# All orders of steps laid out anew, fills over 32 rows, and the latest producer's wait named first, in a four-layer block on one core

## The chip, the cores and the metric

The kernel runs on 1 core of one Trainium2 chip. The metric is the device time of one execution in microseconds, the median of several runs. A core has a matrix engine (TensorE, PE in the profile), a vector engine (VectorE, DVE), a scalar engine (ScalarE, ACT), a general one (GpSimd, POOL), and SyncE (SP), which here only issues DMAs. Each works off its own list of instructions in order; semaphores tie the lists together.

## The reference, cut to what matters

The input x has the shape (16, 64, 64, 256): 16 images of 4096 tokens of 256 values. Four layers follow each other, each on a group norm of x and added to x:

```python
def layer0(x, emb):             # codebook of 1024 vectors
    dis = sum(x*x, -1) + sum(emb*emb, 0) - 2 * x @ emb
    return take(emb.T, argmin(dis, -1))
def layer1(x):                  # within each row of 64 tokens
    f, g, h = x @ Wf + bf, x @ Wg + bg, x @ Wh + bh        # 32, 32, 256 wide
    return einsum('bhij,bhjo->bhio', sigmoid(f @ g.T), h)
def layer2(x):                  # n = 4096 tokens of an image
    x0, x1, x2 = x @ w1, x @ w2, x @ w3
    sm = softmax(x0[:, :, None] * x1[:, None, :], axis=1)
    return sigmoid(einsum('bn,bnm->bm', x2, sm)) * x
def layer3(x):                  # linear attention, 4 heads of 32
    q, k, v = split(x @ w_qkv)
    q, k = softmax(q, over the 32) * 32**-0.5, softmax(k, over tokens)
    out = einsum('context(k, v), q') @ w_out + b_out
    return (out - mean) * rsqrt(var + 1e-3) * gamma + beta
for layer in (layer0, layer1, layer2, layer3):
    x = x + layer(group_norm(x, groups=32))
```

## The kernel before

An image stays in SBUF as XT, 256 channels (two chunks of 128) by 4096 tokens, in 8 groups of 512 tokens. Loads, transposes in and out, the layers' work and the additions are small steps, each a Python function that issues one to a dozen instructions on one engine, waits for what it needs and raises a semaphore when done. A step is called as `exp(old, 7, 1)`: the image, then which piece of it.

**Orders.** For every engine the kernel holds a list of step calls, written out by hand: a prologue for the first image, a loop, and an epilogue. The loop body runs 15 times, with three images in flight: new is turned in, scored (layer 0), put through layer 1 and projected for layer 2; old has its layer 2 (the fills and exps), its gate and the start of layer 3; last gets the end of layer 3 and is sent out. Nothing but these lists decides what stands behind what on an engine; only waits for semaphores tie the engines to each other.

**Stages of one pass through the loop on PE.** First the fill stage: fills, sums, the end of layer 3 of last (final_out, L1515), and turn_in of new (L1273). Then the scoring stage, with fills of old between the scores. Then the gate of old and layer 1 of new, then layer 3 of old with the projection of new.

**Layer 0.** The group norm's factors come from gn(0) (PE L1258 and L1261, DVE, POOL). ACT norms a group (L551) and rounds it to fp16 as n_hi (L567), POOL makes the remainder n_lo (L435). score on PE is, per tile of 128 tokens and half of the codebook, six matmuls by the helper split (L1239: hi hi, hi lo, lo hi for two chunks). best on DVE (L896) adds the bias and takes the maximum of a half, index (L902) finds its place, POOL gathers the code vector (L441), PE turns it (L1297), DVE adds it (L908).

**Layer 1.** Per group ACT norms (L551) and rounds (L578), POOL makes the remainder (L448), PE does l1_fg (L1316), l1_h (by L1239), l1_scores (L1340) and l1_out (L1350), ACT copies fg (L586) and does the sigmoid by tanh (L591, L595), DVE copies h and adds (L916, L923).

**Layer 2.** project writes the three projections of an image as rows; they are split into bfloat16 pieces, 12 rows per quad of partitions that lie 32 apart. The tensors of pieces hold 32 rows per quad: rows 12 to 31 are set to zero at the start (L463, L465) and nothing writes them afterwards. A pair fill(h, 0), fill(h, 1) computes x0 times x1 for one tile and four quads of 512 tokens: two matmuls each (L1407), on 12 rows, the first step on quads 0 and 1, the second on quads 2 and 3. exp on ACT (L618) takes each half from PSUM; sums on PE (L1416) multiplies the four quads' exps with a stationary of 4 columns and gathers into PSUM. A part of the tiles goes by bexp on ACT (L629) and bsum on DVE (L992) instead. The last step is the gate (DVE L999, ACT L639 to L645, PE L1425, L1434).

**Layer 3.** Norm and rounding (ACT L551, L662; POOL L458), l3_qv and l3_k on PE (L1239), exp on ACT, l3_q on DVE (L1030, L1032), the turns on PE (L1461, L1471), the context (L1483). At the end final_out on PE (L1515) turns a group back, DVE (L1088, L1101) and ACT (L695) do the layer norm, POOL the root (L495).

**Waits.** A step names its waits one after the other ahead of its instruction. In the built program the first that is named rides on the instruction itself, and every further one is an instruction of its own ahead of it. In the orders shown below the last name in the brackets is the one that rides.

## Time and profile before

| what | us |
|---|---|
| median of 3 runs | 5465.11 (5464.95 to 5479.77) |
| profiled execution, its own time | 5467.99 |
| its span | 5466.2 |
| PE busy | 5123.3 |
| DVE busy | 4387.4 |
| ACT busy | 4037.1 |
| POOL busy | 1964.2 |
| mean granted clock of PE | 0.963 |

The span is what the profile covers; the execution's own time is 1.8 us more, and 2.9 us more than the median. Busy time is the sum of what an engine's instructions took, without its waits, and matmuls' ends are modelled, so a busy PE may be waiting for its clock. The granted clock is a share of 2.4 GHz. Times in the rows below are from the start of the span. The fifteen passes of the loop repeat about every 331 us; most rows are from one of them, from 2103 to 2434 us. In the rows of stretches each engine has its busy time and, in brackets, its instructions; behind POOL stand the granted clock, the DMA share and GB/s.

### The profile page before, as it was taken

How to read it: one execution, taken by the hardware profiler on the slowest of the kernel's cores; microseconds unless marked ns; L12 is line 12 of the kernel's file. 1: busy time of each engine (PE TensorE's matmuls, PEld its weight loads, DVE VectorE, ACT ScalarE, POOL GpSimd, SP SyncE). 2: the span in 40 equal slices, each digit the busy share in tenths (PEclk: the TensorE clock that was granted, in tenths of full speed). 3: DMA queues.
4: the chain of work that ended last, by engine and by line, in shares of the span. 5: the costliest groups of instructions: out<-in, count | busy, mean ns of one | idle time of the engine just before them, and what ended most of it. 6: DMA issues, size and time to landing. Idle time of an engine off the chain costs nothing.

```text
span 5466.2 us, 109580 instructions
## 1 busy us (share of the span) xinstructions
PE 5123.3 (94%) x42984; PEld 2689.9 (49%) x42984; DVE 4387.4 (80%) x9218; ACT 4037.1 (74%) x6279; POOL 1964.2 (36%) x1594
## 2 busy tenths in 40 slices
PE   7799999999999999999999999999999999999986
PEld 3436445363543646445363553645446464453624
DVE  8478797887878888797887978778798887978836
ACT  1477878678786877868778786787868778786785
POOL 4225143342423425143351423424244351433403
PEclk9899999999999999999999999999999999999988
DMA  2010201102021020211102021020211102011000
GB/s 76 29 37 12 75 27 57 42 7 81 20 71 32 25 65 14 74 29 44 52 8 80 22 67 36 21 66 17 71 32 37 56 11 77 26 62 38 12 31 32
DMA packets 167966, 227.84 MB, mean 42 GB/s; under 512 B 13793, under 2 KB 146657, under 8 KB 167457
## 3 DMA queue, kind: packets, MB, share of 16 engines
q1 hardware_dynamic: 142880, 153.70, 8.5%
q0 software_dynamic: 24576, 67.14, 4.2%
q8 instruction: 345, 5.65, 0.4%
q14 instruction: 165, 1.34, 0.1%
HBM read 153.55 MB, written 67.24 MB: 40 GB/s over the span
## 4 chain that ended last, share of the span: by engine, by line
PE 72%; DVE 13%; ACT 9%; issue 4%; DMA 1%; POOL 1%; DVEq 0%; SPq 0%; ACTq 0%; POOLq 0%
PE PS L1239 36%; PE PS L1416 14%; PE PS L1407 5%; PE PS L1350 3%; PE PS L1515 2%; PE PS L1273 2%; ACT big L618 2%; DVE work L896 2%; PE PS L1297 2%; DVE stats L878 2%; ACT n_x L551 2%; PE PS L1316 1%; DVE idx L902 1%; PE PS L1365 1%; ACT soft L618 1%
## 5 line engine op out<-in xcount | busy, mean ns | idle before, releaser
L618 ACT ACTIVATE big<-PS 128x1024 f32<-128x1024 f32 x1216 | 1207.5, 1028 | 384.7 <-PE PS L1407 350.8
L441 POOL DMA_INDIRECT quant_H<-emb_t,idx x512 | 509.0, 994 | 906.2 <-DVE idx L902 879.7
L1239 PE MATMUL PS<-e_hi,n_hi 128*128 128x512 f16 x2048 | 780.4, 381 | 16.5 <-DVE m L896 9.0
L1239 PE MATMUL PS<-e_lo,n_hi 128*128 128x512 f16 x2048 | 777.2, 379 | 0.0
L1239 PE MATMUL PS<-e_hi,n_lo 128*128 128x512 f16 x2048 | 777.2, 379 | 0.0
L618 ACT ACTIVATE soft<-PS 128x1024 f32<-128x1024 f32 x576 | 577.3, 1030 | 257.8 <-PE PS L1407 255.8
L1416 PE MATMUL PS<-big,w 128*4 128x512 f32 x4864 | 680.3, 646 | 0.0
L878 DVE BATCH_NORM_STATS2 stats<-XT 128x6 f32<-128x512 f32 x1024 | 652.9, 683 | 11.0 <-POOL XT L454 1.0
L902 DVE FIND_INDEX8 idx<-m,work 128x8 uint32<-128x1024 f32 x512 | 624.2, 1219 | 0.0
L1407 PE MATMUL PS<-rhs,lhs 12*128 12x512 bf16 x3584 | 522.8, 403 | 71.5 <-ACT big L618 35.6
L495 POOL TENSOR_TENSOR rstd<-rstd,mhalf 128x4 f32<-128x4 f32 x128 | 131.9, 1030 | 1123.1 <-DVE rstd L1091 1123.1
L896 DVE CUSTOM_DVE_ANT_0 work<-PS,e_bias 128x512 f32<-128x512 f32 x512 | 350.6, 685 | 163.7 <-PE PS L1239 162.5
L1407 PEld LDWEIGHTS PS<-rhs,lhs 12*128 12x128 bf16 x3584 | 126.8, 91 | 677.9 <-ACT big L618 242.2
L551 ACT ACTIVATE n_x<-XT,gt,gs 128x512 f32<-128x512 f32 x512 | 393.6, 806 | 72.9 <-DVE gt L873 70.5
L896 DVE CUSTOM_DVE_ANT_0 work<-PS,e_bias,m 128x512 f32<-128x512 f32 x512 | 379.4, 741 | 32.0 <-PE PS L1239 26.7
L1239 PE MATMUL PS<-qv_hi,o_both 128*128 128x256 f16 x2048 | 357.9, 273 | 21.6 <-DVE soft L1032 21.6
L1239 PEld LDWEIGHTS PS<-e_hi,n_hi 128*128 128x128 f16 x2048 | 199.4, 97 | 351.1 <-DVE m L896 123.8
L435 POOL TENSOR_TENSOR n_lo<-n_x,n_hi 128x1024 f16<-128x1024 f32 x128 | 273.6, 2137 | 259.3 <-ACT n_hi L567 258.2
L992 DVE CUSTOM_DVE_ANT_0 o_x<-o_x,o_both 128x1024 f32<-128x1024 f32 x256 | 311.5, 1217 | 61.8 <-ACT o_x L629 61.8
L454 POOL TENSOR_TENSOR XT<-XT,big 128x1024 f32<-128x1024 f32 x128 | 303.5, 2379 | 151.8 <-DVE big L999 149.9
L629 ACT ACTIVATE o_x<-o_both,negm,s 128x1024 f32<-128x1024 f32 x256 | 317.7, 1241 | 38.7 <-DVE bnum L992 38.7
L448 POOL TENSOR_TENSOR n_lo<-n_x,n_hi 128x1024 f16<-128x1024 f32 x128 | 273.4, 2136 | 160.7 <-ACT n_hi L578 160.7
(214 smaller groups left out, 11030.5 us busy)
## 6 DMA issues: line engine op xcount, KB each, us to landing
xin<-x SPq DMA_DIRECT2D x128, 512.0 KB, 4.3
out<-yout SPq DMA_DIRECT2D x128, 512.0 KB, 3.0
o_both<-rows_d SPq DMA_DIRECT2D x32, 512.0 KB, 7.1
quant_H<-emb_t,idx POOLq DMA_INDIRECT x512, 2.8
XT<-emb SPq DMA_DIRECT2D x1, 1024.0 KB, 6.1
rows_d<-n_hi SPq DMA_DIRECT2D x32, 4.0 KB
XT<-wh SPq DMA_DIRECT2D x1, 256.0 KB, 5.5
XT<-wqv SPq DMA_DIRECT2D x1, 256.0 KB, 5.6
```

What stands on the lines that cost most here:

```text
L441: nc.gpsimd.indirect_dma_start(quant[:, g % 2, u, :], None, emb_t, bass.IndirectOffsetOnAxis(ap=idx[:, t % (2 * GT), 0:1], axis=0),).then_ ...
L454: nc.gpsimd.tensor_tensor(here, here, gated[:, g % 2, :, :], ALU.add).then_inc(g_added.sem, 1)
L551: return nc.scalar.activation(dst, XT[:, im % 2, k, g, :], copy, scale=gs[:, layer, k:k + 1], bias=gt[:, layer, k:k + 1])
L618: nc.scalar.activation(E[h % 3][:, z * 1024:(z + 1) * 1024], bank(2 * z, 2), ACT.Exp).then_inc(exped.sem, 1)
L629: nc.scalar.activation(EB, x0_row, ACT.Exp, scale=s3[:, 1, t:t + 1], bias=negm[:, t:t + 1], accum_out=bden[:, i:i + 1]).then_inc(b_exped.s ...
L878: last = v.bn_stats(stats[:, layer, k, g, :], XT[:, im % 2, k, g, :])
L896: v.tensor_tensor_reduce(biased[:, t % 2, part], bank(5 + half), e_bias[:, part], 1.0, m8[:, t % 2, 0:1] if half else -BIG, ALU.add, ALU.m ...
L902: v.max_index(idx[:, t % (2 * GT), :], m8[:, t % 2, :], biased[:, t % 2, :]).then_inc(l0_indexed.sem, 1)
L992: v.tensor_tensor_reduce(EB, EB, x2_row, 1.0, 0.0, ALU.mult, ALU.add, bnum[:, i:i + 1]).then_inc(b_summed.sem, 1)
L1239: ins = mm(dst, a, b, start=first and j == 0, stop=last and j == 2)
L1407: ins = mm(bank(r), lhs[rr, t * P:(t + 1) * P], rhs[rr, f * GW:(f + 1) * GW], start=True, stop=True)
L1416: ins = mm(PS[32 * q:32 * q + 4, 4, :], w2[:, t, f, :], E[h % 3][:, q * 512:(q + 1) * 512], start=h == 0, stop=h == HALVES - 1, skip_group ...
```

## The change

Three things are changed.

1. Every list of step calls of the five engines, in prologue, loop and epilogue, is written in another order. The sets of steps stay the same.
2. fill takes 32 rows of each quad instead of 12. The added rows are the zeros of the pieces, so the result is the same.
3. In some sixteen steps the waits are named in another order, so that the one for the producer expected last is first and rides on the instruction; score waits for l0_lo only at the first tile of a group, instead of at every tile, which takes 384 waits off PE.

The diff of the steps, cut: where a step is not shown in full, one or two waits changed places in the same way. Of the lists one line stands for all.

```diff
@@ SP, loop
-                exp(old, 0, 0); rows_back(old); final_out(last, 1); final_out(last, 3); turn_in(new, 1)
+                exp(old, 0, 0); rows_back(old); turn_in(new, 1); final_out(last, 1); turn_in(new, 3)
...
@@ ACT, l0_norm
-                    act.wait_ge(*l0_scored.room(im, 2 * (g * GT + GT) - 1, 4 * GT))
                     act.wait_ge(*l0_xn.after(im, g))
+                    act.wait_ge(*l0_scored.room(im, 2 * (g * GT + GT) - 1, 4 * GT))
@@ ACT, l1_norm
-                act.wait_ge(*l1_hed.room(im, 2 * g + 1, 4))
                 act.wait_ge(*l1_xn.after(im, g))
+                act.wait_ge(*l1_hed.room(im, 2 * g + 1, 4))
@@ ACT, l3_norm (l3_qved.room) and l3_qv (l3_ctxed.room): behind the other wait
...
@@ DVE, best
                 if half == 0:
+                    dve.wait_ge(*l0_scored.after(im, 2 * t))
                     dve.wait_ge(*l0_indexed.room(im, t, 2))
                 else:
                     dve.wait_ge(*l0_maxed.after(im, 2 * t))
-                dve.wait_ge(*l0_scored.after(im, 2 * t + half))
+                    dve.wait_ge(*l0_scored.after(im, 2 * t + 1))
@@ DVE, gating (g_normed), qsoft (l3_qturned.room), l3_q (l3_qsoft.room), final_sq (f_sq)
...
@@ DVE, final_out
+                dve.wait_ge(*f_turned.after(im, c))
...
-                dve.wait_ge(*f_turned.after(im, c))
@@ PE, score
-                pe.wait_ge(*l0_maxed.room(im, 2 * t + half, 2))
-                if half == 0:
-                    if im + t == 0:
-                        pe.wait_ge(emb_squared, 1)
+                if half == 0 and t % GT == 0:
                     pe.wait_ge(*l0_lo.after(im, g))
+                pe.wait_ge(*l0_maxed.room(im, 2 * t + half, 2))
+                if im + t + half == 0:
+                    pe.wait_ge(emb_squared, 1)
@@ PE, turn0 (l0_added.room), l1_fg (l1_tanhed.room), l1_h (l1_hkept.room): behind the other wait
...
@@ PE, fill
-                    rr = slice(32 * r, 32 * r + PIECES)
+                    rr = slice(32 * r, 32 * r + 32)
@@ PE, l3_k
-                pe.wait_ge(*l3_kexped.room(im, g, 1))
...
+                pe.wait_ge(*l3_kexped.room(im, g, 1))
@@ PE, l3_qv
-                pe.wait_ge(*l3_qsub.room(im, g, 1))
...
+                pe.wait_ge(*l3_qsub.room(im, g, 1))
```

**Where the order moves, on PE.** The fill stage of a pass in the middle of the loop, around the sums of half 13 of old; L1407 is a fill (x2 one step, x4 two), L1416 the sums, L1273 turn_in, and in the changed kernel L1409, L1418, L1274 and L1517 (final_out). Before:

```order
L1239 MATMUL PS<-m_hi,n_x 128x256
L1407 MATMUL PS<-rhs,lhs 128x512 x2
L1416 MATMUL PS<-big,w 4x512 x4
L1407 MATMUL PS<-rhs,lhs 128x512 x2
L1273 MATMUL PS<-ident,xin 128x128 x4
L1407 MATMUL PS<-rhs,lhs 128x512 x2
L1416 MATMUL PS<-soft,w 4x512 x4
L1273 MATMUL PS<-ident,xin 128x128 x4
```

And now:

```order
L1240 MATMUL PS<-m_hi,n_x 128x256
L1409 MATMUL PS<-rhs,lhs 128x512 x2
L1418 MATMUL PS<-big,w 4x512 x4
L1418 MATMUL PS<-soft,w 4x512 x4
L1409 MATMUL PS<-rhs,lhs 128x512 x4
L1274 MATMUL PS<-ident,xin 128x128 x4
L1517 MATMUL PS<-ident,XT 128x128 x4
L1240 MATMUL PS<-m_hi,quant_H 128x256
```

Two sums now stand together, and two fill steps stand in one block of four matmuls where they stood apart. The turns that lay between single fills come behind the block.

**On ACT,** layer 1 of a pass: L551 is a norm in two halves (into o_x and xin for the gate of old, into n_x for layer 1 of new, all by the same helper), L578 the rounding of n_x, L586 the copy of fg, L591 and L595 the sigmoid. Before:

```order
L551 ACTIVATE o_x<-XT,gt,gs 128x512 x2
L586 ACTIVATE work<-PS,fg_bias 64x256 x2
L551 ACTIVATE n_x<-XT,gt,gs 128x512 x2
L578 ACTIVATE n_hi<-n_x 128x1024
L551 ACTIVATE xin<-XT,gt,gs 128x512 x2
L591 ACTIVATE work<-PS 128x256
L595 ACTIVATE attn<-work,ones 64x4x64 x2
L586 ACTIVATE work<-PS,fg_bias 64x256 x2
L551 ACTIVATE o_x<-XT,gt,gs 128x512 x2
L591 ACTIVATE work<-PS 128x256
L595 ACTIVATE attn<-work,ones 64x4x64 x2
L551 ACTIVATE n_x<-XT,gt,gs 128x512 x2
```

And now:

```order
L551 ACTIVATE o_x<-XT,gt,gs 128x512 x2
L586 ACTIVATE work<-PS,fg_bias 64x256 x2
L551 ACTIVATE xin<-XT,gt,gs 128x512 x2
L591 ACTIVATE work<-PS 128x256
L595 ACTIVATE attn<-work,ones 64x4x64 x2
L586 ACTIVATE work<-PS,fg_bias 64x256 x2
L551 ACTIVATE n_x<-XT,gt,gs 128x512 x2
L578 ACTIVATE n_hi<-n_x 128x1024
L551 ACTIVATE n_x<-XT,gt,gs 128x512 x2
L578 ACTIVATE n_hi<-n_x 128x1024
L551 ACTIVATE o_x<-XT,gt,gs 128x512 x2
L591 ACTIVATE work<-PS 128x256
```

The first pair of norm and rounding is that of group 4: it moves behind a gated product, a sigmoid and a copy of fg, and the pair of group 5 follows it directly.

**On DVE,** the reduction of a first and a second half score in the scoring stage, with its waits (L896 before, L897 now; L992 is bsum). Before:

```order
L896 ISA work,m<-PS,e_bias 128x512 [waits l0_scored,l0_indexed]
L896 ISA m 128x1
L896 ISA work,m<-PS,e_bias,m 128x512 [waits l0_scored,l0_maxed]
L896 ISA m 128x1
L992 ISA o_x,bnum<-o_x,o_both 128x1024 [waits b_exped]
```

And now:

```order
L897 ISA work,m<-PS,e_bias,m 128x512 [waits l0_scored,l0_maxed]
L897 ISA m 128x1
L903 MAX_INDEX idx<-m,work 128x8 [waits l0_maxed]
L897 ISA work,m<-PS,e_bias 128x512 [waits l0_indexed,l0_scored]
L897 ISA m 128x1
```

In the first half (no m among its operands) the wait for the score now rides; in the second half the order of the two stays.

## Rows read from the trace of the kernel before

**Rows 1.** The page: its span, then busy time of the engines (share) xinstructions.

```profile
span 5466.2 us, 109580 instructions
...
PE 5123.3 (94%) x42984; PEld 2689.9 (49%) x42984; DVE 4387.4 (80%) x9218; ACT 4037.1 (74%) x6279; POOL 1964.2 (36%) x1594
```

**Rows 2.** Busy time by stage of one image: stretch, length, PE, PEld, DVE, ACT, POOL, granted clock.

```profile
2103.00:2157.00 54.00, 52.30 (x665) 44.15 (x666) 48.82 (x80) 49.14 (x80) 38.15 (x18) 1.00 0.01 2
2157.00:2212.00 55.00, 50.66 (x619) 37.84 (x617) 45.94 (x99) 35.17 (x60) 23.27 (x31) 1.00 0.01 2
2212.00:2293.00 81.00, 77.91 (x615) 32.55 (x615) 59.96 (x130) 76.49 (x140) 8.07 (x8) 0.96 0.35 115
2293.00:2306.00 13.00, 12.16 (x62) 2.25 (x62) 3.98 (x13) 10.12 (x13) 2.83 (x2) 0.61 0.04 15
2306.00:2409.00 103.00, 102.99 (x597) 42.99 (x594) 96.59 (x212) 64.73 (x85) 42.13 (x34) 1.00 0.12 35
2409.00:2434.00 25.00, 21.79 (x135) 7.30 (x133) 18.30 (x46) 16.30 (x19) 7.58 (x7) 0.93 0.10 28
...
5190.00:5346.00 156.00, 130.42 (x844) 35.44 (x845) 52.32 (x117) 140.19 (x216) 10.79 (x8) 0.86 0.08 28
```

**Rows 3.** Timeline, end of the turn_in stage: start us, length, engine line op shapes.

```profile
2287.08 0.39 PE L1407 MATMUL PS<-rhs,lhs 12*128 12x512 bf16 x4
...
2287.40 0.66 PE L1273 MATMUL PS<-ident,xin 128*128 128x128 f32 x4
...
2289.47 0.66 PE L1515 MATMUL PS<-ident,XT 128*128 128x128 f32 x4
...
2290.23 0.87 DVE L1101 SCALAR_TENSOR_TENSOR yout<-soft,rstd,PS 128x256 f32<-128x256 f32 x2 [0.18 <-PE PS L1515]
...
2291.03 0.39 PE L1407 MATMUL PS<-rhs,lhs 12*128 12x512 bf16 x2
...
2291.35 0.66 PE L1273 MATMUL PS<-ident,xin 128*128 128x128 f32 x4
...
2292.05 0.69 DVE L884 COPY XT<-PS 128x512 f32<-128x512 f32 x1 [0.94 <-PE PS L1273]
```

**Rows 4.** Timeline of PE and DVE late in the scoring stage.

```profile
2410.02 0.38 PE L1239 MATMUL PS<-e_hi,n_lo 128*128 128x512 f16 x1
...
2410.54 0.69 DVE L896 CUSTOM_DVE_ANT_0 work<-PS,e_bias 128x512 f32<-128x512 f32 x1
```

**Rows 5.** Page: costliest groups, the first half of each score (L896), idle time last.

```profile
L896 DVE CUSTOM_DVE_ANT_0 work<-PS,e_bias 128x512 f32<-128x512 f32 x512 | 350.6, 685 | 163.7 <-PE PS L1239 162.5
```

**Rows 6.** Timeline of ACT in layer 1: group 6's norm and its rounding.

```profile
2134.85 1.52 ACT L551 ACTIVATE n_x<-XT,gt,gs 128x512 f32<-128x512 f32 x2
2136.46 1.06 ACT L578 ACTIVATE n_hi<-n_x 128x1024 f16<-128x1024 f32 x1
```

**Rows 7.** Who waited for whom on PE: us in total, times, longest.

```profile
PE PS L1239 <- DVE soft L1032: 21.6, 47, 0.7
```

**Rows 8.** Granted clock (third number from the end) around the first fills; one image, then another.

```profile
2210.40:2213.80 3.40, 2.52 (x46) 1.48 (x46) 3.20 (x6) 3.09 (x6) 0.00 (x0) 1.00 0.02 5
2213.80:2217.20 3.40, 3.21 (x46) 1.55 (x48) 1.34 (x6) 2.90 (x5) 0.00 (x0) 0.51 0.00 0
...
893.00:900.00 7.00, 5.14 (x97) 2.92 (x98) 5.85 (x13) 5.91 (x9) 0.00 (x0) 1.00 0.00 1
```

**Rows 9.** Timeline: an exp behind slow PE, the first group's remainder, the first score.

```profile
2219.37 1.02 ACT L618 ACTIVATE soft<-PS 128x1024 f32<-128x1024 f32 x1 [1.34 <-PE PS L1407]
...
2301.88 2.13 POOL L435 TENSOR_TENSOR n_lo<-n_x,n_hi 128x1024 f16<-128x1024 f32 x1 [4.10 <-ACT n_hi L567]
...
2306.07 0.39 PE L1239 MATMUL PS<-e_hi,n_hi 128*128 128x512 f16 x1
```

## What I expect, and why

> **What bounds the kernel.** I read the busy times of the page first, then the busy times by stage, then timelines at the borders of stages. TensorE (PE) is busy 94% of the span, VectorE (DVE) 80%, ScalarE (ACT) 74% [rows 1]. PE does the bulk of every stage, but a re-ordering can gain only where PE stands still, works longer than it must, or is slow because of its clock. The stages of one image, which repeats 15 times with a period of 331 us, tell them apart [rows 2]. While the codes are scored (2306 to 2409) PE is busy 102.99 of 103 us at the full granted clock: nothing to win but work left out. In the fill stage before it (2212 to 2293) PE has 77.91 and ACT 76.49 of 81 us, so both press. In layer 1 (2103 to 2157) PE has 52.30, ACT 49.14 and DVE 48.82 of 54 us. The rest is lost at three borders where the granted clock falls: 0.96 over the 81 us of the fill stage, 0.61 over the 13 us before the scores, 0.93 over the last 25 us [rows 2].
>
> **Part 1, which wait rides on the instruction.** The built program puts the wait that a step names first on the instruction itself and every further one into an instruction ahead of it. What that costs when the late producer stands in the separate one: the last product of a half score ends at 2410.02 + 0.38 = 2410.40 and the reduction starts at 2410.54, 0.14 us later [rows 4]; a final_out starts 0.10 us after its transposes (2289.47 + 0.66, then 2290.23) [rows 3]. Where the only wait rides on the instruction, turn_in's copy starts at 2292.05 after 2291.35 + 0.66 = 2292.01, 0.04 us [rows 3]. So a wake by a late producer gets 0.06 to 0.10 us shorter. ACT's rounding after its own norm starts 0.09 us after it (2134.85 + 1.52, then 2136.46) [rows 6] and gets some 0.06 us. The group of first halves idles 163.7 us in 512 runs, 0.32 each [rows 5], so many of them do wait. DVE and ACT together win more than that, but only wakes on PE's path count. I take 7 per image (three half scores, two final_outs, some ACT norms; a choice, since these stages alternate between engines) at 0.09 us: 0.6 us. Against it: in l3_qv PE waits for DVE's subtraction, 21.6 us in 47 times [rows 7], and that wait moves off the instruction; 3 of these per image at 0.06 us give 0.2 back, which leaves **0.4 us** per image. Bounds: 0 and, with 15 such wakes, 1.2 us. The 384 waits of PE that are dropped (l0_lo on three of four tiles) had long been met; I cost them at nothing, since in the scoring stage PE shows no idle that they could fill.
>
> **Part 2, blocks of fills.** A block of four matmuls of L1407 (two fill steps) holds PE from 2287.08 to 2287.40, 0.32 us, and a block of two from 2291.03 to 2291.35, again 0.32 us [rows 3]. The second step of a pair is free. Counted in the order of PE, the fills of one image in the loop stand in 70 blocks before and in 67 after. PE is freed of 3 x 0.32 = 1.0 us per image, nearly all in the fill stage, where ACT lacks only 4.5 of 81 us [rows 2]. So half of it, **0.5 us**, is my value; 0 and 1.0 are the bounds.
>
> **Part 3, fills over 32 rows.** The duration: the transposes of [rows 3] on 128 rows and the fills on 12 rows show no price per row that I can separate; the second step of a pair costs nothing although it uses other rows. I take 0. The clock is another matter. Before a fall PE's work at these borders is mostly fills on 12 rows, small matmuls and waiting. At 2210.4 PE is busy 2.52 of 3.4 us, and then its clock falls to the lower level, 1.2 GHz (0.51 over the next 3.4 us); in another image PE is busy 5.14 of 7 us at the same place, 73% against 74%, and stays at 2.4 GHz [rows 8]. Busy time does not tell the two apart, so what is in it does, and rows that a matmul drives are a candidate. What a fall costs: at the first fills an exp waits 1.34 us for a slow fill (2219.37); with a shorter wait of the exp before it I take up to 1.8 us. Before the scores n_lo of the first group is there at 2301.88 + 2.13 = 2304.01, but PE, still at its slow sums, starts the first score at 2306.07: 2.0 us [rows 9]. At the third border POOL's n_lo comes last anyway: 0. All three gone would be 3.9 us per image. The first border is low in about half of the images, the others in nearly all. If more rows count at all, the first border, with many fills, recovers first, and the one before the scores, where sums on 4 columns make up much of the work, only sometimes. I take 0.9 + 0.1 for these: **1.0 us** per image. Bounds 0 (below nothing only if more active rows cost clock, and nothing in the trace shows that) and 3.0 us.
> The Trainium skill, "TensorE: Matmul & The Clock Gate", section "What's actually happening", says that the clock is set by how busy PE has been recently. By that alone 12 or 32 rows would be the same and this term 0. The two stretches of [rows 8] speak against busy time as the whole of it, but do not show that rows are what is missing.
>
> **Part 4, the new orders.** Orders of the scoring stage keep the number of scores, sums and fills, and PE is full there. In layer 1 ACT's norm and rounding of group 4 (1.52 + 1.06 = 2.6 us by the same pair of [rows 6]) move behind the next gated, tanh and fg, and group 5's directly behind it, while PE's l1_h(4, 0) moves ahead of two spreads. Group 4 gets later, group 5 earlier. In layer 3 DVE now takes both steps of gn(2) in a row, and stands still while PE runs an l3_qv between them. ACT and DVE have 5 to 9 us to spare in these stages [rows 2], so I expect most to be covered and put **0.3 us** per image against it, between 0 and 2.6. The prologue hardly changes. The last image's fill stage is ACT's (140.19 of 156 us, PE 130.42) [rows 2]; its blocks of fills fall from 62 to 58 without a gain, since ACT needs the fills no sooner. I leave it at 0, give or take 10 us.
>
> **The sum.** Per image 0.4 + 0.5 + 1.0 - 0.3 = 1.6 us; by 15 images 24 us, and about 3 us from the last image's borders, which have the same falls (0.86) [rows 2]: 27 us. The profiled execution took 5467.99 us around its span of 5466.2; that gives 5441. The median of the runs is 2.9 us lower, so the median after should be 5465.1 - 27 = **5438 us**, 0.5% faster.
>
> **Rivals.**
> *Rows do not count for the clock.* Then the falls stay, 16 us of the sum go, and the time is about 5454, within 0.3%. For it: busy share is what one would expect to count. Against it: [rows 8].
> *The falls nearly all go.* 3.0 us instead of 1.0, and shorter low stretches in the last image: 5438 - 35 = 5403. For it: the same 8 matmuls of fills stand before each fall. Against it: before the scores the sums, unchanged, make most of PE's time.
> *The gains are off the path.* Where ACT and PE press together, the shorter wakes and blocks turn into idle time, and new small waits eat the rest: 5462. For it: the fill stage's 76.49 against 77.91.
> *New waits in layer 1 and 3.* PE reaches l1_h(4, 0) earlier and its operand comes 2.6 us later. If nothing covers that, it is 2.6 x 15 = 39 us; less 12 for shorter wakes and blocks it ends at 5492. It is slower than before by more than can be measured once the new waits exceed some 1.9 us per image. For it: ACT has only 4.9 us to spare in this stage. Against it: group 5, later in the chain, comes earlier by about as much.
>
> **Chances.** The forecast 0.45, no clock gain 0.13, falls gone 0.12, off the path 0.13, new waits 0.17. A measurement of this kernel tells about 0.3%, 16 us, from no change: faster than 5449 in forecast and falls gone, 0.57; within it 0.26; slower 0.17. The range goes from 5395 to 5482: it takes in most of the falls-gone case and the two without a change, and leaves about 0.2 outside, mostly above.
>
> **What would show it.** Right: the granted clock at the first fills stays at 1.00 in more images, the stage before the scores shows 0.7 or more, L896's first half idles 0.1 us less each time, DVE's wakes after transposes shrink to 0.04 us. Wrong: PE waits on n_lo (L448 of before) in layer 1, or on gn(2) before project; ACT's waits for fills grow; the mean clock stays at 0.963.

## The result, and the profile after

The changed kernel takes 5512.52 us in the median (5507.99 to 5519.55, 4 runs), the kernel before 5469.75 us in the same comparison: a ratio of 1.0073, 95% interval 1.0056 to 1.009. It is 40 us slower where 27 us less were forecast, and outside the range. The profiled execution took 5508.5 us around a span of 5506.7.

Two points of the description above need setting right. The orders of the prologue are the same in both kernels, and so is POOL's list in the epilogue; the other lists differ, with the same sets of steps. And the zeros of rows 12 to 31 are not written once at the start: POOL writes them anew for every image (L463 and L465), in both kernels alike. So the 32 rows need no new instruction.

The first lines of the page of the changed kernel, and some of its groups (busy, mean ns of one, idle time just before them). They answer to [rows 1] and [rows 5].

```profile
span 5506.7 us, 109196 instructions
...
PE 5080.7 (92%) x42984; PEld 2702.1 (49%) x42984; DVE 4481.0 (81%) x9218; ACT 4025.2 (73%) x6279; POOL 1970.9 (36%) x1594
...
L897 DVE CUSTOM_DVE_ANT_0 work<-PS,e_bias 128x512 f32<-128x512 f32 x512 | 348.6, 681 | 123.6 <-PE PS L1240 123.6
L993 DVE CUSTOM_DVE_ANT_0 o_x<-o_x,o_both 128x1024 f32<-128x1024 f32 x256 | 351.0, 1371 | 96.2 <-ACT o_x L629 94.4
```

PE is busy 43 us less although it has the same 42984 matmuls, and its mean granted clock went from 0.963 to 0.971: the clock rose, as forecast. The first halves of the scores (L897) idle 0.24 us each instead of 0.32; e2 and e3 below show that only half of this comes from the waits. But DVE is busy 94 us more with the same 9218 instructions. One group of it, bsum (L993), takes 1371 ns where it took 1217.

The same pass by stage (stretch, length, PE, PEld, DVE, ACT, POOL, granted clock), from layer 1 to the gate, with borders at the stages' first matmuls; it answers to [rows 2].

```profile
2125.54:2182.54 57.00, 55.17 (x664) 46.83 (x661) 50.51 (x80) 48.29 (x79) 38.62 (x18) 0.97 0.01 2
2182.54:2239.95 57.41, 50.31 (x601) 36.56 (x600) 47.83 (x96) 34.97 (x60) 22.39 (x30) 0.97 0.01 2
2239.95:2315.45 75.50, 73.07 (x609) 31.88 (x613) 58.64 (x127) 73.71 (x137) 8.08 (x8) 1.00 0.37 120
2315.45:2327.72 12.27, 10.56 (x74) 1.89 (x73) 4.98 (x16) 11.82 (x15) 2.84 (x2) 0.86 0.13 43
2327.72:2440.52 112.80, 111.35 (x636) 46.35 (x633) 107.03 (x230) 66.97 (x87) 45.87 (x37) 1.00 0.12 35
2440.52:2458.78 18.26, 15.82 (x121) 4.88 (x118) 10.47 (x28) 14.25 (x17) 4.74 (x4) 0.81 0.06 20
```

With the borders set in every pass by the same matmuls, the mean lengths of the 15 passes are (us):

| kernel | fill stage | to the scores | scoring | to layer 1 | layer 1 | layer 3 | pass |
|---|---|---|---|---|---|---|---|
| before | 78.3 | 12.9 | 111.2 | 18.2 | 55.6 | 52.9 | 329.1 |
| changed | 75.4 | 12.6 | 112.9 | 17.9 | 56.0 | 57.6 | 332.5 |
| e1, rows | 77.2 | 12.3 | 111.2 | 18.2 | 55.8 | 52.9 | 327.5 |
| e2, waits | 80.6 | 12.3 | 110.9 | 17.6 | 55.3 | 52.9 | 329.5 |
| e3, orders | 78.5 | 13.0 | 111.3 | 18.1 | 55.7 | 57.5 | 334.1 |
| e5, rows and waits | 77.0 | 11.9 | 110.9 | 17.9 | 55.8 | 52.9 | 326.4 |
| e7, bsum moved | 75.7 | 12.5 | 111.2 | 17.8 | 55.7 | 57.4 | 330.2 |
| e8, two moves | 75.8 | 12.3 | 113.0 | 17.6 | 55.3 | 54.0 | 328.0 |
| e12 | 75.4 | 12.3 | 111.2 | 17.9 | 55.6 | 52.9 | 325.3 |

Over the 15 passes the changed kernel gains 44 us in the fill stage, 3 ahead of the scores and 5 ahead of layer 1, and loses 26 in the scoring stage, 5 in layer 1 and 71 in layer 3. Outside the passes it gains 9. That makes, before rounding, the 40.5 us between the two spans. So the loss has two places. (Some expectations below give layer 3 as 50.5 against 55.2 us: there it ends at its last l3_qv, 2.4 us earlier.) The lengths come from one profiled execution of each kernel. Executions of one kernel differ, above all in the clock: those of the kernel before ran from 5460 to 5490 us at mean clocks of 0.956 to 0.965, and the profiled one, at 0.963, is among the faster ones.

**Layer 3.** PE's matmuls of the changed kernel that stood still longest there (start, length, idle time before and who ended it):

```profile
2192.07 0.59 PE L1240 MATMUL PS<-o_both,k_hi 128*128 128x512 f16 x2 [1.51 <-ACT soft L666]
...
2208.89 0.27 PE L1378 MATMUL PS<-ident,mm 128*2 128x128 f32 x1 [0.95 <-DVE mm L954]
2210.97 0.48 PE L1380 MATMUL PS<-dg,ones 2*128 2x2 f32 x2 [1.81 <-DVE dg L957]
2211.39 1.11 PE L1463 MATMUL PS<-ident,soft 128*128 128x128 f32 x4
```

L1378 and L1380 are PE's turns for the extremes of the projections: DVE reduces the columns, PE turns them (L1378), DVE reduces again and makes dg, and PE spreads it (L1380). The last row is four turns that take 1.11 us here and 0.66 where the clock is full. The clock falls in 11 of the 15 passes, always between 27.7 and 29.1 us into layer 3, that is at the extremes, never behind the first wait; in the kernel before it does not fall in this stage at all. What a fall costs can be read from the passes themselves (from the first l3_qv to the first fill, 0.2 us more than in the table): layer 3 takes 56.0 us in the four passes without low clock, 57.6 in the three with 3.4 us of it, 58.8 in the eight with 6.8 us. The kernel before takes 53.1. So of the 4.7 us lost per pass 3.0 are lost at full clock, and 1.7 by the clock.

DVE at the first of the places, and POOL beside it:

```profile
2187.76 0.77 DVE L855 BATCH_NORM_AGGREGATE mv<-stats 128x2 f32<-128x48 f32 x2
2188.56 1.95 DVE L859 TENSOR_TENSOR dm<-mv,beta_c 128x2 f32<-128x2 f32 x1
2190.43 0.68 DVE L1009 TENSOR_REDUCE kneg<-PS 128x1 f32<-128x512 f32 x1
```

```profile
2188.36 2.13 POOL L458 TENSOR_TENSOR o_both<-o_x,o_both 128x1024 f16<-128x1024 f32 x1 [7.72 <-ACT o_both L662]
```

L859 works on two numbers per partition. It starts 0.20 us after POOL's remainder and ends with it, at 2190.51 against 2190.49. In the kernel before it takes 0.16 us. L1009, whose result ACT's exp (L666) waits for, stands directly behind it: that is PE's 1.51 us. At the extremes it is a division of the second l3_qsoft_ that stands ahead of the columns and is held in the same way (0.69 us elsewhere), and then dg itself (L957, 0.22 us elsewhere):

```profile
2205.78 2.08 DVE L1018 TENSOR_TENSOR soft<-soft,qsum 128x512 f32<-128x512 f32 x1
...
2209.51 1.41 DVE L957 TENSOR_SCALAR dg<-ident,mt 2x2 f32<-2x2 f32 x1
```

**The scoring stage.** DVE and PE of the changed kernel:

```profile
2416.18 3.87 DVE L993 CUSTOM_DVE_ANT_0 o_x<-o_x,o_both 128x1024 f32<-128x1024 f32 x1
...
2416.79 2.16 POOL L435 TENSOR_TENSOR n_lo<-n_x,n_hi 128x1024 f16<-128x1024 f32 x1
...
2418.97 0.38 PE L1240 MATMUL PS<-e_hi,n_lo 128*128 128x512 f16 x1
...
2419.98 0.68 DVE L897 CUSTOM_DVE_ANT_0 work<-PS,e_bias 128x512 f32<-128x512 f32 x1
...
2420.72 0.39 PE L1240 MATMUL PS<-e_hi,n_hi 128*128 128x512 f16 x1 [1.37 <-DVE m L897]
```

The bsum, 1.2 us long elsewhere, lasts until 1.1 us after POOL's operation. It is bsum 14 in each of the 15 passes, 3.86 us in the mean, and the 15 others are at 1.2. The next best comes late, and PE's score after 2419.35 waits 1.37 us for it, in a stage that had no idle time to give.

Taken together, DVE's operations that are held while POOL works are 143 us longer over the changed kernel than their usual lengths, and 47 us in the kernel before. The difference, 96 us, is the 94 us that DVE is busy more.

### The profile page after: what moved, and what is told of

It reads as the page before. It is cut to its first block, busy times and chain, and to the rows that moved or that the text cites. A ratio compares the mean times of both kernels' runs of the same rounds, so it can differ in the third digit from the quotient of the medians.

```text
span 5506.7 us, 109196 instructions
## 1 busy us (share of the span) xinstructions
PE 5080.7 (92%) x42984; PEld 2702.1 (49%) x42984; DVE 4481.0 (81%) x9218; ACT 4025.2 (73%) x6279; POOL 1970.9 (36%) x1594
## 4 chain that ended last, share of the span: by engine, by line
PE 56%; DVE 20%; ACT 14%; issue 6%; DMA 2%; POOL 1%; SPq 0%; DVEq 0%; ACTq 0%
PE PS L1240 29%; PE PS L1418 9%; PE PS L1409 4%; ACT big L618 4%; PE PS L1352 3%; DVE idx L903 3%; DVE work L897 3%; ACT soft L618 3%; ACT n_x L551 2%; PE PS L1318 2%; PE PS L1274 2%; DVE stats L878 2%; PE PS L1299 1%; DMA out<-yout 1%; PE PS L1517 1%
## 5 line engine op out<-in xcount | busy, mean ns | idle before, releaser
L441 POOL DMA_INDIRECT quant_H<-emb_t,idx x512 | 521.0, 1017 | 959.9 <-DVE idx L903 925.1
L1418 PE MATMUL PS<-big,w 128*4 128x512 f32 x4864 | 649.1, 616 | 0.5 <-ACT big L618 0.5
L1409 PE MATMUL PS<-rhs,lhs 32*128 32x512 bf16 x3584 | 502.3, 392 | 85.9 <-ACT soft L618 40.7
L495 POOL TENSOR_TENSOR rstd<-rstd,mhalf 128x4 f32<-128x4 f32 x128 | 131.1, 1024 | 1095.3 <-DVE rstd L1092 1095.3
L1409 PEld LDWEIGHTS PS<-rhs,lhs 32*128 32x128 bf16 x3584 | 124.8, 91 | 694.8 <-ACT big L618 267.2
L897 DVE CUSTOM_DVE_ANT_0 work<-PS,e_bias 128x512 f32<-128x512 f32 x512 | 348.6, 681 | 123.6 <-PE PS L1240 123.6
L551 ACT ACTIVATE n_x<-XT,gt,gs 128x512 f32<-128x512 f32 x512 | 392.5, 808 | 59.1 <-DVE gt L873 57.0
L993 DVE CUSTOM_DVE_ANT_0 o_x<-o_x,o_both 128x1024 f32<-128x1024 f32 x256 | 351.0, 1371 | 96.2 <-ACT o_x L629 94.4
L897 DVE CUSTOM_DVE_ANT_0 work<-PS,e_bias,m 128x512 f32<-128x512 f32 x512 | 380.0, 742 | 52.4 <-PE PS L1240 46.1
L435 POOL TENSOR_TENSOR n_lo<-n_x,n_hi 128x1024 f16<-128x1024 f32 x128 | 274.7, 2146 | 214.2 <-ACT n_hi L567 213.0
L448 POOL TENSOR_TENSOR n_lo<-n_x,n_hi 128x1024 f16<-128x1024 f32 x128 | 273.3, 2135 | 139.3 <-ACT n_hi L578 139.3
```

What stands on the lines that cost most here:

```text
L441: nc.gpsimd.indirect_dma_start(quant[:, g % 2, u, :], None, emb_t, bass.IndirectOffsetOnAxis(ap=idx[:, t % (2 * GT), 0:1], axis=0),).then_ ...
L551: return nc.scalar.activation(dst, XT[:, im % 2, k, g, :], copy, scale=gs[:, layer, k:k + 1], bias=gt[:, layer, k:k + 1])
L897: v.tensor_tensor_reduce(biased[:, t % 2, part], bank(5 + half), e_bias[:, part], 1.0, m8[:, t % 2, 0:1] if half else -BIG, ALU.add, ALU.m ...
L993: v.tensor_tensor_reduce(EB, EB, x2_row, 1.0, 0.0, ALU.mult, ALU.add, bnum[:, i:i + 1]).then_inc(b_summed.sem, 1)
L1409: ins = mm(bank(r), lhs[rr, t * P:(t + 1) * P], rhs[rr, f * GW:(f + 1) * GW], start=True, stop=True)
L1418: ins = mm(PS[32 * q:32 * q + 4, 4, :], w2[:, t, f, :], E[h % 3][:, q * 512:(q + 1) * 512], start=h == 0, stop=h == HALVES - 1, skip_group ...
```

## The experiments

Each ratio is to the kernel before on the same chip.

**e1: the rows alone.**

```diff
-                    rr = slice(32 * r, 32 * r + PIECES)
+                    rr = slice(32 * r, 32 * r + 32)
```

> The kernel before with one edit: a fill drives 32 rows instead of 12; orders and waits stay. Theory (rows count for the granted clock): the low clock at the first fills and ahead of the scores goes as it went in the changed kernel (there from 78 + 113 us of low clock in the loop to 34 + 41), each fall saved gives about 2 us, so 25 to 45 us less than before, about 5430, mean clock 0.970 or more. Rival 1 (the new orders kept the clock up, not the rows): clock 0.963 and the time of before within 5 us. Rival 2 (32 rows cost time themselves): the fills' mean goes above 403 ns and the time above that of before.

Measured: 0.9934 (0.9921 to 0.9947), 36 us less, within the 25 to 45 expected. The mean clock of its executions is 0.970 to 0.975, against 0.957 to 0.963 of the kernel before beside it, and a fill takes 395 ns in the mean instead of 403, so the added rows cost no time. The first 10 us of fills of two passes, of the kernel before and then of e1 (the granted clock is the third number from the end):

```profile
2212.10:2222.10 10.00, 9.53 (x78) 2.77 (x82) 6.44 (x24) 8.14 (x11) 0.00 (x0) 0.66 0.39 138
2543.10:2553.10 10.00, 9.56 (x82) 2.74 (x82) 6.40 (x24) 8.14 (x11) 0.00 (x0) 0.66 0.41 143
```

```profile
2208.20:2218.20 10.00, 9.07 (x89) 2.98 (x89) 6.74 (x26) 9.98 (x13) 0.00 (x0) 1.00 0.50 177
2535.70:2545.70 10.00, 9.08 (x89) 2.97 (x89) 6.74 (x26) 9.98 (x13) 0.00 (x0) 1.00 0.48 148
```

PE does more matmuls in less busy time (at the low clock each takes longer), ACT is busy 9.98 us of the 10 instead of 8.14. The low clock, added up over the 15 passes from the records of the granted clock, goes from 78 to 20 us in the fill stage, where it appears in 9 of 15 passes before and in 3 of e1, and from 113 to 79 ahead of the scores. Low clock is the lower of its two levels, 1.2 GHz. Nothing but the number of rows differs. The Trainium skill, "TensorE: Matmul & The Clock Gate", section "What's actually happening", makes the clock depend on how busy PE has been. The trace does not agree if that means the busy time that a profile shows: in the 3 us around the first fill, before the clock falls in the one and stays in the other, PE is busy for the same time. First the kernel before, then e1:

```profile
2210.10:2213.10 3.00, 2.04 (x44) 1.40 (x44) 2.83 (x6) 2.69 (x6) 0.00 (x0) 1.00 0.02 5
```

```profile
2206.20:2209.20 3.00, 2.05 (x44) 1.40 (x44) 2.83 (x6) 2.69 (x6) 0.00 (x0) 1.00 0.03 5
```

**e2: the waits alone,** on the orders and rows of before (for instance):

```diff
                 if half == 0:
+                    dve.wait_ge(*l0_scored.after(im, 2 * t))
                     dve.wait_ge(*l0_indexed.room(im, t, 2))
```

> The kernel before with one edit: the waits in their new order (and l0_lo on one tile of four); orders and 12 rows stay. Theory: wakes get 0.06 to 0.10 us shorter, of which little is on PE's path: 0 to 15 us less than before. Rival (the new waits are what made the changed kernel slow, since some late ones now stand apart, as l3_qsub on PE): 20 to 70 us slower than before, with layer 3 longer than 50.5 us an image.

Measured: 0.9991 (0.9982 to 1.0), 5 us less, at the edge of what can be told from nothing; the rival is refuted. What a wait that rides is worth is seen where DVE waits for the same score, first of the kernel before, then of e2 (its lines are 911 and 1265):

```profile
2332.16 0.38 PE L1239 MATMUL PS<-e_hi,n_lo 128*128 128x512 f16 x1
...
2332.69 0.69 DVE L896 CUSTOM_DVE_ANT_0 work<-PS,e_bias 128x512 f32<-128x512 f32 x1 [0.41 <-PE PS L1239]
```

```profile
2341.04 0.38 PE L1265 MATMUL PS<-e_hi,n_lo 128*128 128x512 f16 x1
...
2341.46 0.69 DVE L911 CUSTOM_DVE_ANT_0 work<-PS,e_bias 128x512 f32<-128x512 f32 x1 [0.37 <-PE PS L1265]
```

The reduction starts 0.15 us behind the product before and 0.04 in e2. That is so in each of the 121 first halves of a kernel that found DVE waiting, and the second halves, whose waits kept their order, stay at 0.15 in both: 0.11 us a wake. Since only 121 of the 512 wait in this way, the group's idle time falls by no more than 19 us, 163.7 to 145.0, or 0.04 us each.

In the profiled executions e2 gains 0.3 to 0.6 us per pass in each of the stages from the one ahead of the scores to layer 1, and loses 2.3 in the fill stage, where the low clock rose from 78 to 195 us. That rise is in good part real, since the mean clock over all executions is 0.957 in the median against 0.960, but its size rests on one execution of each. PE's wait for the subtraction, which now stands apart, rose from 21.6 to 23.5 us in 47 times, 0.04 us each; layer 3 is no longer for it.

**e3: the orders alone.**

> The kernel before with one edit: all orders of steps as in the changed kernel; waits and 12 rows as before. Theory (the orders bring the loss: 71 us in layer 3 and 26 us in the scoring stage over the loop, and the rows hide part of it): slower than the changed kernel by what the rows and waits give, 5525 to 5550, with bsum 14 at 3.9 us and gn(2)'s first operation at 1.9 us as in the changed kernel. Rival (rows or waits bring the loss): 5470 or less.

Measured: 1.0127 (1.011 to 1.0143), 69 us more, 5545 us in the median and so within the expectation. Layer 3 is at 57.5 us, as long as in the changed kernel. Of the detail one half holds, gn(2)'s first operation is long, and one fails, the bsum is not. DVE and POOL of e3 at the same place (their lines are 1006 and 437 here):

```profile
2420.37 1.22 DVE L1006 CUSTOM_DVE_ANT_0 o_x<-o_x,o_both 128x1024 f32<-128x1024 f32 x1
...
2421.04 2.56 POOL L437 TENSOR_TENSOR n_lo<-n_x,n_hi 128x1024 f16<-128x1024 f32 x1
```

The order on DVE is the same as in the changed kernel. POOL's operation starts 0.67 us after the bsum instead of 0.61 (0.66 to 0.67 over the passes against 0.61 to 0.63), and now POOL is the one that takes longer (2.56 instead of 2.14), bsum takes its 1.22, and the scoring stage is 111.3 us. So the loss in the scoring stage needs the new orders and the new waits together (with the old orders and new waits, e2 and e5, it is 110.9), and hangs on hundredths of a microsecond. The first halves idle 143.2 us here, with the old waits: the orders alone take 0.04 us off each, as much as the waits alone.

**e4: the changed kernel with the old orders in layer 3.** In the loops of PE, DVE and ACT the part from the start of layer 3 is that of before (for instance DVE):

```diff
-                l1_out(new, 7); l3_q(old, 0); l3_kturn(old, 0); gn(new, 2, 0); l3_k(old, 1)
+                l1_out(new, 7); gn(new, 2, 0); l3_q(old, 0); l3_k(old, 1); l3_kturn(old, 0)
...
```

> The changed kernel, but in the loop the orders of PE, DVE and ACT from the start of layer 3 to the end of the body as before. Theory (late columns and gn(2) on DVE, and DVE's operations that meet POOL's, make PE wait there, and the clock falls behind the waits): layer 3 takes 50.5 to 51.5 us again instead of 55.2, no low clock in it, 60 to 70 us less than the changed kernel: about 5445. Rival (layer 3 is longer by its waits, which stand in another order, or by what layer 1 leaves it): it stays at 53 us or more, and the time above 5480.

Measured: 0.9924 (0.9911 to 0.9937), so 81 us less than the changed kernel by the two ratios (69 by the spans). By the ratios that is more than the 60 to 70 expected, by the spans it is within it. Layer 3 is 52.9 us, with no low clock. The place is layer 3 and its cause is the order in it.

**e5 and e6: both edits of the steps on the old orders, and the changed kernel with 12 rows.**

> The kernel before with both edits of the steps (32 rows, new order of waits) and the old orders. The two alone gave -0.66% and -0.09%. Theory (independent): -0.75%, about 40 us less than the kernel before of the same chip, low clock in the fill stage near 20 us over the loop as with the rows alone. Rival (the new waits bring idle time at the first fills, where the low clock went from 78 to 195 us with them alone, and undo part of what the rows give): -0.5% or less.

Measured: 0.9911 (0.9897 to 0.9925). The two alone make -0.75% and together -0.89%, with -0.75% at the edge of the interval. The low clock in the fill stage is 20 us: with 32 rows the waits no longer cost there. The changed kernel is this one with the new orders, and it is 1.6% or 89 us slower: that is the price of the orders on top of the other two edits.

> The changed kernel with fills on 12 rows again. Theory: the rows give 0.6% on these orders too, so 1.0134 to 1.015 of the kernel before, with 150 us or more of low clock in the fill stage. It also tells whether bsum 14 (3.7 us in the changed kernel, 1.2 us with the new orders and old waits) is long by the waits (then 3.7 here) or by the rows (then 1.2).

Measured: 1.0121 (1.0105 to 1.0136). The rows give 0.48% here, somewhat less than the 0.6% expected. The low clock in the fill stage is 96 us instead of the 150 expected, and in the changed kernel it is 34. bsum 14 takes 3.9 us, as in the changed kernel: the waits, not the rows, put it into POOL's way.

**e7: bsum 14 moved.**

```diff
-                best(new, 24, 1); bsum(old, 14); best(new, 25, 0); add0(new, 10); index(new, 24); best(new, 25, 1)
+                best(new, 24, 1); best(new, 25, 0); add0(new, 10); index(new, 24); best(new, 25, 1); bsum(old, 14)
```

> The changed kernel with one step moved in DVE's loop: bsum(old, 14) stands behind best(new, 25, 1) instead of behind best(new, 24, 1), so it starts when POOL's remainder of that group (89.1 to 91.2 us after the first score) is over. Theory (bsum 14 takes 2.6 us longer because POOL's operation runs at the same time, best is late, and PE stands still 1.37 us in the scoring stage): every bsum takes 1.2 us, the scoring stage 111.0 to 111.4 us instead of 112.9, 20 to 27 us less than the changed kernel, ratio to before 1.0025 to 1.0035. Rival (the scoring stage is longer by the new waits or by where scores and fills stand): bsum gets short, the stage stays at 112.5 or more.

Measured: 0.9997 (0.9986 to 1.0008). Every bsum is at 1.2 us, and the scoring stage of the pass is full again:

```profile
2310.24:2421.32 111.08, 111.08 (x636) 46.40 (x633) 104.58 (x230) 66.97 (x87) 45.87 (x37) 1.00 0.13 36
```

The stage gains 26 us over the 15 passes, as expected, and the spans differ by 31. The ratios make it 41, more than the expectation, with intervals of some 6 and 9 us on the two. One step, moved by four places.

**e8, e9, e10: two moves on DVE in layer 3, and each alone.**

```diff
-                l1_out(new, 7); l3_q(old, 0); l3_kturn(old, 0); gn(new, 2, 0)
+                l1_out(new, 7); gn(new, 2, 0); l3_q(old, 0); l3_kturn(old, 0)
...
-                l3_qsoft_(old, 1); l3_qsoft_(old, 2); columns(new); extremes(new); l3_kturn(old, 2)
+                l3_qsoft_(old, 1); columns(new); extremes(new); l3_kturn(old, 2)
...
-                l3_ctx(old, 1); l3_q(old, 3)
+                l3_ctx(old, 1); l3_q(old, 3); l3_qsoft_(old, 2)
...
```

> The changed kernel with two steps moved in DVE's layer 3, the rest as it is: gn(new, 2, 0) directly behind l1_out(new, 7), ahead of the first q of old, and l3_qsoft_(old, 2) behind l3_q(old, 3), so that it no longer stands ahead of columns and extremes. Theory (these two places make PE wait for gn(2) and for the extremes, and the clock falls there): the two operations of 1.9 and 2.1 us take 0.2 and 0.7, layer 3 takes 51 to 53 us instead of 55.2, 30 to 60 us less than the changed kernel. Rival (the orders of PE and ACT in layer 3 bring the loss, which went away with all three): less than 15 us.

Measured: 0.9942 (0.9926 to 0.9958), 1.3% or 72 us less than the changed kernel, more than the 30 to 60 expected. Layer 3 of the pass, first of the changed kernel (at full clock), then of e8, and in e8 the operation of gn(2) and PE's turn for the extremes:

```profile
2514.84:2570.70 55.86, 48.76 (x601) 35.77 (x600) 47.62 (x96) 35.08 (x60) 22.38 (x30) 1.00 0.01 2
```

```profile
2483.74:2537.75 54.01, 48.87 (x602) 35.75 (x600) 45.24 (x96) 34.97 (x60) 22.86 (x30) 1.00 0.01 2
```

```profile
2486.85 0.16 DVE L859 TENSOR_TENSOR dm<-mv,beta_c 128x2 f32<-128x2 f32 x1
...
2507.46 0.27 PE L1384 MATMUL PS<-ident,mm 128*2 128x128 f32 x1
2508.35 0.38 PE L1386 MATMUL PS<-dg,ones 2*128 2x2 f32 x2 [0.62 <-DVE dg L957]
```

PE's busy time is that of the changed kernel and DVE's is 2.4 us less, with the same instructions: what left was waiting. In this pass, at full clock in both, that is 1.85 us; the mean gain of 3.6 us a pass holds the low clock as well, of which none is left. The wait for dg is 0.62 us as in the kernel before.

> The changed kernel with one step moved in DVE's loop: gn(new, 2, 0) directly behind l1_out(new, 7). With the second move (l3_qsoft_) as well it was 1.3% less than the changed kernel, layer 3 51.7 us an image instead of 55.3. Theory (of PE's three long waits in layer 3 of the changed kernel, 1.5 us behind the first context and 0.95 + 1.8 us at the extremes, this move takes the first, and what it starts earlier carries the extremes along): a third to two thirds of it, 20 to 45 us less than the changed kernel, and the operation L859 of 1.95 us takes 0.2. Rival (only the columns matter): within 10 us of the changed kernel.

Measured: 1.0017 (1.0005 to 1.0028), 31 us less than the changed kernel. Layer 3 is 1.8 us shorter per pass, about the 1.79 us that L859 was too long, and PE's wait of 1.51 us is gone. But the expectation that the extremes would be carried along failed: their waits stay at 0.9 and 1.8 us, and so does most of the low clock (51 us over the passes).

> The changed kernel with the other step moved alone: l3_qsoft_(old, 2) behind l3_q(old, 3), so not ahead of columns and extremes. Theory (it stands there for 0.55 + 0.7 + 0.25 + 2.1 = 3.6 us, and PE waits 0.95 us behind the extremes' first turn and 1.8 us for the second): 25 to 50 us less than the changed kernel, low clock in layer 3 of 65 us gone for the most part. Rival (gn(2) comes too late anyway, and PE takes the wait elsewhere): within 10 us of the changed kernel.

Measured: 1.0007 (0.9995 to 1.0019), 36 us less. Layer 3 is 2.0 us shorter per pass, and its low clock is gone (65 to 0 us). Nearly all of the gain is the clock: all 15 passes of e10 take 55.8 us where the passes of the changed kernel without low clock take 56.0. The waits at the extremes are shorter by 2 us, but PE takes it up elsewhere, as the rival said: its waits for L666 rise from 22.6 us in 15 times to 30.7 in 30, and those for DVE's copy L1048 from 2.9 in 2 to 15.2 in 17. The two moves are worth 0.56% and 0.66% alone and 1.31% together.

**e11 and e12: all three moves, and the old layer 3 with the bsum moved.**

> The changed kernel with all three moves on DVE: bsum(old, 14), gn(new, 2, 0), l3_qsoft_(old, 2). Theory (the places are independent): the 26 us of the scoring stage and the 70 us of the other two add up, ratio to before 0.987 to 0.990, 5405 to 5422, below the kernel before with both edits of the steps (0.9911). Rival (one engine takes up the slack and the falls of the clock come back): 0.992 or more.

Measured: 0.9906 (0.9888 to 0.9925), just above the expected band and below its rival. By their profiled executions, against e8 the scoring stage gives its 26 us, but the passes keep only 14 of them: 11 go in layer 1 and the stage before it, where the low clock is higher again (51 against 7 us). That rests on one execution of each, and e8's had the highest clock of its own (0.984, of 0.977 to 0.984). What brings the low clock back was not tried.

> The changed kernel with layer 3 in the old orders and bsum(old, 14) moved. The first alone gave 0.9924 of before. Theory: less another 0.5%, 0.986 to 0.989, and about the same as the three moves on DVE, since layer 3 is 50.5 us in the one and 51.7 in the other, and the low clock ahead of the scores is lower in the other. Rival (the new orders ahead of layer 3 fit only the new layer 3): 0.991 or more.

Measured: 0.9877 (0.9856 to 0.9897), 5408 us. It beats both kernels, by 1.2% and 1.9%: the rows, the waits, the new orders ahead of layer 3, the old ones in it, and one step out of POOL's way. Against e5 (0.9911), which has all the old orders, it is 0.3% less, with intervals that just touch: that is what is left of the new orders ahead of layer 3 and in the epilogue once this step is moved.

## Why the prediction was wrong

**Part 1, the waits: right.** A wake got 0.11 us shorter, just above the 0.06 to 0.10 that [rows 3, 4] gave. The sign that I named, 0.1 us less idle time for each first half, was wrong, since it took each of the 512 to be such a wake: the waits took off 0.04, and the 0.08 of the changed kernel has as much from the orders. The whole is 5 us alone (0 to 10 by its interval) and 13 with 32 rows, against 6. The wakes of l3_qv that I charged cost 1.9 us over the kernel, against 2.7. What I missed is that the waits alone raised the low clock in the fill stage of before.

**Part 2, the blocks: not separable.** The orders bring 1.6 us per pass in the fill stage and lose 0.7 ahead of the scores (e5 against the changed kernel), against 0.5 forecast. Blocks and other moves come together in that.

**Part 3, the rows: right in mechanism, too small.** Forecast 18 us. The runs give 36 by e1's ratio and 26 by e6 against the changed kernel; the spans of before and e1 differ by 26. By e1's stages it is 1.1 us per pass at the first fills, against 0.9 forecast; 0.6 ahead of the scores, against 0.1; and 3 us at the end, as forecast. So the first border recovers first, as reasoned from [rows 8], and the term that was mis-sized is the one ahead of the scores. The rival without a clock gain is refuted.

**Part 4, the orders: the step that failed.** It put 0.3 us per pass against the change, 2.6 at most; measured are 69 us alone, 4.6 per pass, and 89 on top of the rows and waits, 5.9 per pass. What the term left out are two things that the runs show: DVE's operations that POOL holds up, and the clock that falls behind PE's new waits. In layer 3 of the changed kernel 1.6 to 1.8 us per pass are L859 held by POOL and the exp late behind it (e9), 1.7 the low clock behind the extremes' waits (e10), and about 1.3 other moves in the orders, of which some 0.2 is the second l3_qsoft_ at full clock and the rest was not taken apart (layer 3 is 52.9 us in e4 and 54.0 in e8). In the scoring stage 1.7 us are bsum 14 held by POOL (e7). Three sentences of it were wrong.
- "ACT and DVE have 5 to 9 us to spare in these stages, so I expect most to be covered." [rows 2] does give DVE 9 us of 55 in layer 3. But the extremes are a chain PE, DVE, PE, and there what stands ahead of a step in DVE's queue makes PE wait, however much is idle elsewhere. DVE's list of the new order has a second l3_qsoft_ ahead of the columns; its price came by the clock. It also has l3_q and l3_kturn ahead of gn(2, 0), but there PE did not wait for gn(2) itself: gn(2, 0) now starts beside POOL's remainder, and the reduction behind it, for PE's next context, is late. I had named gn(2), but its second half, and priced it within 0.3.
- I looked at layer 1, where the pair of norms moved. There PE's wait for the remainder (n_lo for l1_fg), one of my signs of being wrong, is 10.7 us in ten times (6.3 in one before), and layer 1 is 0.4 us longer per pass. The rival *new waits in layer 1 and 3* had the right sign, and its mechanism holds for the stage that it did not price. Its 5492 is 20 us too low.
- "Orders of the scoring stage keep the number of scores, sums and fills, and PE is full there", and "nothing to win". A full stage has nothing to win and everything to lose: 1.4 us of PE's waiting for a late best went straight into the time.

Behind all three lies what I never asked: which of DVE's operations run while POOL works. In one pass of the kernel before two of DVE's small operations (L867, L959) are long for it, and no bsum. The new orders keep L867, let L959 go and put L859, L957 and two of the divisions of l3_qsoft_ (L1018 now) there, and with the new waits bsum 14.

**The clock's own sign.** [rows 8] compared PE's busy share in stretches of different length and place (3.4 and 7 us) to say that busy time does not tell a pass with a fall from one without. With equal stretches around the first fill, as shown under e1, it is the same (2.04 of 3 us), so the conclusion holds there.

## What to carry to other kernels

When an order is laid out anew, lay DVE's operations with two operands in SBUF against POOL's tensor operations: more than half of what the orders cost here came from two such meetings (L859 and bsum 14). Then take the chains that go to another engine and come back (a global extreme) and count what stands ahead of each link in its queue; idle time of the stage does not cover them, and a wait of PE can cost more in the clock behind it than in itself. When small matmuls stand near idle time, try filling their empty rows with zeros: it cost nothing here, and the clock fell less often.

## What the runs showed of the hardware

**DVE and POOL exclude each other for some operations.** POOL's remainders (L435, L448, L458: 128x1024 elements, 2.13 us) hold up DVE operations with two operands in SBUF that start while they run. The small ones end with the remainder: L859 takes 1.95 us instead of 0.16, in all 15 passes. The divisions L1018 end 0.55 us behind it. A DVE operation with a tensor in PSUM is not touched, as L924 of the changed kernel, at its usual 0.75 us within POOL's 2178.50 to 2180.64:

```profile
2178.50 2.14 POOL L458 TENSOR_TENSOR o_both<-xin,o_both 128x1024 f16<-128x1024 f32 x1 [0.36 <-ACT o_both L662]
```

```profile
2179.50 0.75 DVE L924 SCALAR_TENSOR_TENSOR XT<-PS,beta_c,XT 128x512 f32<-128x512 f32 x1
```

Nor is one with a single tensor in SBUF (L1014, 0.68 us inside and outside a remainder). POOL's gathers (L441) do not matter: 74 bsums beside them take 1.2 us. Nor do its operations that write zeros: L1018 takes its usual 0.69 us within L465's 2.27, in all 15 passes. It goes the other way round as well: POOL's root (L495, 128x4) takes 1.91 us instead of 1.01 where a bsum started 0.17 us ahead of it. The Trainium skill, "SBUF — State Buffer", section "SBUF: two separate sides", has this as an exclusive lock on a shared port pair, for DVE operations with two SBUF inputs against a GpSimd operation that reads SBUF. The traces agree, but for one thing: it gives the pair to whichever starts first, and bsum 14 was recorded 0.61 us ahead of POOL's operation and still waited it out; at 0.67 us ahead (e3) it did not. What happens in those 0.6 us stays open.

**The granted clock stays up with 32 rows where it falls with 12.** Zeros on 20 more rows per quad took the low clock in the fill stage from 78 to 20 us over the passes, with the same instructions and the same busy time of PE around the first fill (2.04 and 2.05 of 3 us). With the new orders it went from 96 to 34 us (e6 and the changed kernel). By what the chip decides this the runs cannot tell.
